# A ring of twenty slots in place of ten for the nodes' own rows in the two source walks

## The reference, cut to what matters

```python
# edge_index = [src, dst]; loops (node, node) are appended to it
h = jax.ops.segment_sum(norm[:, None] * x[col], row, num_segments=num_nodes)
xp = (1.0 - ALPHA) * h + ALPHA * x
```

## Time and profile before

| | |
|---|---|
| median of 3 runs | 5597.37 us (5596.43 to 5601.04) |
| profiled execution, its own time | 5592.3 us |
| its span, from first to last instruction | 5590.6 us |
| e0: first gather to start of the last matmul | 396.0 to 653.1 us |
| e1a: the same | 1015.0 to 1300.5 us |
| e1b: the same | 1302.8 to 1590.6 us |

### The profile page before, as it was taken

One profiled execution on the slowest core, in us unless ns is written; L12 is line 12 of the kernel. 1 busy time (PEld: TensorE's weight loads), 2 busy tenths in 40 slices (PEclk: granted clock), 3 DMA queues, 4 the chain that ended last, 5 costly groups with the idle time before them and its releaser, 6 DMA issues. The chain is left out here.

```text
span 5590.6 us, 101447 instructions
## 1 busy us (share of the span) xinstructions
PE 3616.3 (65%) x21453; PEld 2519.8 (45%) x21454; DVE 3365.2 (60%) x13936; ACT 2238.3 (40%) x6392; POOL 3611.4 (65%) x4923
## 2 busy tenths in 40 slices
PE   4527799777788489968959999930006996200298
PEld 3427688666666244432226666620005775100033
DVE  6434477443468577777758888850806886244288
ACT  0005477666667333323328888700003442000155
POOL 2747566675735377725648888876574555757698
PEclk8659999999999799988979999955558998555699
DMA  1015577687889552200114444352017885411398
GB/s 29 1 33 161 161 240 236 199 244 213 238 241 285 188 196 53 53 18 28 35 59 144 137 144 139 128 153 53 31 41 239 291 290 179 118 34 41 127 342 300
DMA packets 551031, 816.76 MB, mean 146 GB/s; under 512 B 118566, under 2 KB 267629, under 8 KB 550466
## 3 DMA queue, kind: packets, MB, share of 16 engines
q1 hardware_dynamic: 396820, 559.50, 31.8%
q0 software_dynamic: 69184, 122.90, 9.0%
q10 hardware_dynamic: 84816, 132.30, 6.4%
HBM read 493.48 MB, written 329.46 MB: 147 GB/s over the span
## 5 line engine op out<-in xcount | busy, mean ns | idle before, releaser
L620 POOL DMA_INDIRECT agg_dst<-e_rows,e_put_i x392 | 390.3, 996 | 203.8 <-issue 118.8
L1867 POOL DMA_INDIRECT e_rows<-h,e_other_i x392 | 388.6, 991 | 148.5 <-issue 118.8
L1209 POOL TENSOR_TENSOR n_rstd<-n_rstd,minus_half 128x4 f32<-128x4 f32 x294 | 333.5, 1134 | 23.1
L689 POOL DMA_INDIRECT agg<-e_msg,e_put_i x196 | 194.1, 990 | 224.1 <-DVEq L718 172.8
L1222 ACT ACTIVATE n_o<-n_y_ps,n_shift,n_rstd 128x128 f32<-128x128 f32 x784 | 294.5, 463 | 11.6 <-POOL n_shift L1482 11.0
L364 POOL DMA_INDIRECT by_src<-s_pay_s,s_place_i x196 | 188.3, 961 | 112.5 <-issue 58.8
L937 PE MATMUL e1b_bank<-y_rows,e1b_hot 128*128 x1584 | 205.9, 291 | 81.7 <-ACT e1b_bank L1049 58.4
L1683 POOL DMA_INDIRECT lg_rows<-x,e_other_i x196 | 187.5, 956 | 109.7 <-issue 59.4
L895 POOL DMA_INDIRECT x_rows<-x,d_other_i x196 | 185.9, 948 | 112.0 <-issue 59.1
L2366 POOL TENSOR_TENSOR n_u<-n_u 128x512 f32<-128x512 f32 x98 | 124.5, 1270 | 205.2 <-DVE n_u L2313 205.2
L937 PE MATMUL e1a_bank<-y_rows,e1a_hot 128*128 x1584 | 206.4, 291 | 78.3 <-ACT e1a_bank L1035 52.1
(11 more groups left out here) (513 smaller groups left out, 11950.0 us busy)
## 6 DMA issues: line engine op xcount, KB each, us to landing
n_ag<-agg_dst SPq DMA_DIRECT2D x294, 264.0 KB, 3.6
n_xs<-x SPq DMA_DIRECT2D x294, 256.0 KB, 3.4
n_hs<-h SPq DMA_DIRECT2D x196, 264.0 KB, 3.9
agg_dst<-e_ev SPq DMA_DIRECT2D x196, 132.0 KB
y<-n_o ACTq DMA_DIRECT2D x98, 264.0 KB, 3.1
e1a_fed<-y SPq DMA_DIRECT2D x196, 132.0 KB
m<-e1a_ev SPq DMA_DIRECT2D x196, 132.0 KB
e1b_fed<-m SPq DMA_DIRECT2D x196, 132.0 KB
```

The costliest lines, as they stand in the source:

```text
L620: pool.indirect_dma_start(out=agg, out_offset=bass.IndirectOffsetOnAxis(ap=e.put_i[:, c:c + 1], axis=0), in_=rows[:, c, :], in_offset=None ...
L689: pool.indirect_dma_start(out=agg, out_offset=bass.IndirectOffsetOnAxis(ap=e.put_i[:, c:c + 1], axis=0), in_=msg[:, g % SLOTS, k, 0:out_wi ...
L1209: st(pool.tensor_tensor(rstd, rstd, keep.minus_half[:, :], ALU.pow))
L1867: pool.indirect_dma_start(out=rows[:, c, :], out_offset=None, in_=h, in_offset=bass.IndirectOffsetOnAxis(ap=e.other_i[:, c:c + 1], axis=0))\
```

## The change

The ring `fed` gets twenty slots, each with a semaphore of its own, in place of ten. FED stands in the ring's size, in the slot and count of each load and wait, in the number of loads before the loop, and in which tile is asked for after a take.

```diff
-EV, FED = 4, 10
+EV, FED = 4, 20
```

## The result

The changed kernel takes 5535.8 us (median of 4 runs, 5532.5 to 5538.5); the kernel before, run beside it and earlier, 5596.9 (4 runs, 5585.7 to 5601.0). The ratio is 0.9895, interval [0.9879, 0.991]. The two medians are 61.1 us apart; by the ratio the gain is 58.8 us of the 5597, and 48.5 were forecast. The profiled execution takes 5536.55 us after 5592.3, a gain of 55.8.

The account below looks back on a forecast made before the run. The prediction took ACT's waits for tile-row loads, led by only three tiles, to bound e1a and e1b. A ceiling of 59.1 us less 2.6, 6 and 2 gave 48.5, so 5549 us; 8-in-10 range 5537 to 5582.

Parts of the forecast that it names:

- My account of the lateness: Walks e1a and e1b: a load lands in 3.2 us, three tiles of ACT cover 2.5 us, so ACT waits.
- The ceiling of 59.1 us: Most the change could gain: time beyond the gathers, 28.4 us in e1a and 30.7 us in e1b.
- What is lost of it: Parts of the 59.1 us not won in e1a and e1b: 2.6, 6 and 2 us, leaving 48.5.
- the 2.6 us for late landings at the end: Last gathers of e1a and e1b land later beside loads than in e0: 1.3 us lost a walk.
- the 8 us for the middle of the walks: Loss of 6 us from ACT and PE waiting for one another, plus 2 us from e1b's standstills.
- e1b's three stalls: ACT stands still about 4.66 us three times at a turn's end; between nothing and 4.7 us remains, 2 taken.
- What is next behind: After the load waits go, POOL's gathers at 4.99 us a round bound e1a and e1b, ahead of ACT, PE, SP, DMA.
- (a): ACT without load waits: 229 us in e1a, 18 us inside the gathers; 235 us in e1b, 12 inside.
- The forecast of share and rate: DMA engines in the middle of e1a: share 95%, traffic about 267 GB/s, fitting narrowly.
- The rival of full engines: DMA engines already full at a share of 0.86 to 0.88; gain 0 to 10 us, about 5594 us; chance 0.11.
- The eviction ring: Rival: stores landing in 4.07 us make rounds 5.35 us; gain 36 us in all, 5561 us; chance 0.24.
- The burst: Rival: ten more loads at a walk's start delay first gathers, 6.7 us a walk, 5611 us; chance 0.05.

Follow-up runs that it names:

- e1: Changed kernel with twenty slots kept but loads asked for only ten tiles ahead, as before: 6862.7 us against 6864.1, ratio 0.9997 (second kind of chip).
- e3: Ring of 8 slots, so a lead of one tile: 7146.6 us, ratio 1.0411 to the kernel before (second kind).
- e2: Changed kernel with twenty slots but loads asked for twelve tiles ahead, a lead of five: 6846.8 us, ratio 0.9971 to the kernel before (second kind).
- e0: Not a run: the earliest of the kernel's three walks, same sum over as many tiles and chunks as the other two; 260 us in the kernel before.
- e9: Changed kernel, unedited, repeated beside the kernel before on another chip: 5541.0 us against 5595.4, ratio 0.9902 (first kind).
- e4: Changed kernel with ten eviction slots in place of four, in all three walks: 6842.6 us, ratio 0.9968 to the kernel before (second kind).
- e7: Changed kernel with ACT loading the closing values at every second tile in place of every fourth: 6877.9 us, one run (second kind).
- e11: Changed kernel with a lead of five tiles, run once more: 6891.6 us, ratio 0.997 to the kernel before (second kind).
- e12: Changed kernel with ten eviction slots, run once more: 6888.5 us, ratio 0.9968 to the kernel before (second kind).
- e8: Kernel before, with ten eviction slots in place of four: 6899.4 us beside 6896.4, one run (second kind).
- e10: Changed kernel with all 196 gathers of walk e1b left out: 5525.9 us, one run (first kind).
- e5: Changed kernel with half of e1b's gathers left out: 6745.5 us, one run; kernel before 6896.4 (second kind).

## Why the prediction was right, and where not

**What bounded the walks.** Shown. The load of a tile's own rows came late because its lead of three tiles was too short. e1 takes the added lead away and keeps the ring: nothing is won. e3 shortens it: 283 us are lost. e2 stretches it to five: all that a lead can give is there. These three ran only on the second kind, whose walks proper have no gathers beside; on the first kind the cause rests on the traces, in which the load waits and the excess over e0 went together, twice (the result and e9). My account of the lateness left out a part: I set 3.2 us of landing against 2.5 of three tiles. In the earlier trace rows SP issues the load 1.2 us after the start of the take, so it is there after 4.4 us, and ACT is ready for it after 3.1; the 1.3 between them are the wait. e1 shows that the part matters.

**The ceiling of 59.1 us.** It came from the difference of e1a and e1b to e0. The walks now take 258.6 and 260.0 us where e0 took 257.1, so 54.7 were won in the profiled execution and, by the same rows before, 57.1 in e9's.

**What is lost of it.** This is the term that was mis-sized: 10.6 forecast, 4.4 and 2.0 measured. From last gather to the start of the last matmul e1a and e1b now take 13.7 and 15.8 us, where e0 took 12.7; that is 4.1 of the 4.4 us, and 1.6 of e9's 2.0. So the 2.6 us for late landings at the end (3.47 less 2.06 us, twice, is rather 2.8) were about right, and the 8 us for the middle of the walks weren't lost. I gave 3 us a walk to ACT and PE waiting for one another and 2 us to e1b's three stalls. e1b's stalls are still there in the trace after (ACT waits 4.50, 4.66 and 4.78 us, put down to PE, where it waited 4.66, 4.63 and 3.85), and yet e1b gained more than e1a; that the banks in hand and the spare time of a round take them up is my reading, and wasn't tried.

**What is next behind.** Right in kind, wrong in size. I put ACT at 4.5 and PE at 4.53 us a round and called both a tenth below the gathers. Each was the engine by itself, and ACT's from a single round of 4.55. Together, through eight banks and batches of six steps, they make 4.73 in e1a with no gathers (second kind) and 4.86 in e1b (first kind; on the second 4.78 to 4.88 in e2, e4, e7, e11 and e12, which start 477 to 467 ACT instructions from 2100 to 2290 us). The sum in (a) had said so: 229 and 235 us over 49 rounds are 4.67 and 4.80. e7 shows that ACT's own part isn't the limit of that pair; what is, inside it, stays open. e0 is no different: on the second kind its round without gathers is 4.85 to 4.94 us (324 to 330 ACT instructions, two a tile, from 740 to 940 us in e1 to e8). So e0 too, which I called bound by the gathers, is bound by them by only 1 to 3%. A next step that sped up the gathers alone would find 8 us in e1b by e10, and no more.

**DMA.** The forecast of share and rate, 0.95 and 267 GB/s, met 0.93 and 269. The rival of full engines at a share of 0.88 is refuted. The Trainium skill's 358 GB/s (DMA: Bandwidth & Descriptors, Specifications) is 89 above what the walk reached; whether it or the share would have been the wall, no run here shows.

**The eviction ring.** This rival's sign came, with 16.5 and 20.9 us of waits, and its price didn't: the walks end with the gathers. On the second kind ten slots in place of four change nothing (e4 against e2), but there the waits that they remove are 7.0 us, in e1b alone. On the first kind, with 3% of slack, that the waits cost nothing is argued from the walks' lengths and wasn't tried.

**The burst.** Refuted by the trace after: the third batch came 0.6 us earlier.

## What to carry to other kernels

A prefetch must lead by the whole time from the event that frees its issue to its landing, measured against the consumer's fastest burst, not its mean pace: here 1.2 us until SP issues and 3.2 us to land against 0.82 us a tile, where the mean tile took 1.43. Past that, further lead buys nothing: without gathers five tiles did what thirteen did. Beside the gathers five tiles would give 3.1 + 2 x 0.82 = 4.8 us for the 4.4, by my estimate from the earlier trace rows; that wasn't run. So size the lead from the trace and keep the memory. And the pace of two engines that wait for one another isn't that of the slower one alone: take it from a run in which the third is left out, as in e10, before you call a bound clear.

## What the runs showed of the hardware

The same program takes about 5596 us on some chips and 6864 to 6914 on others. In the walks the difference lies in stretches in which POOL issues indirect gathers, and the 35 us behind them: there (e1) PE started 75 matmuls in 200 us where it starts some 1290 without gathers, and ACT and SP fell likewise, while POOL keeps 1.27 us a gather on the mean (1.25 on the first kind); the granted clock of TensorE is 0.50 (its level of 1.2 GHz), with PE busy 27 of the 200 us. Without gathers the pace is that of the first kind (4.78 to 4.88 us a round in e1b, and 4.86 in e10). With half the gathers (e5) the walk was 130 us shorter. By e1's trace the three walks hold 675 of the 1266 us; the rest lies in other phases, which aren't read here. What makes it so stays open; no walk in a trace of the first kind shows any of it. Whoever times a kernel with many gathers should first see which kind of chip it ran on, and then compare two numbers.

A load of 132 KB on SP's queue landed in 3.2 us beside gathers. The Trainium skill's fit for a DMA, 2.0 us plus the bytes over 436 GB/s (DMA: Bandwidth & Descriptors, Anatomy of one DMA), is made for POOL's path and gives 2.3 us for this size, as an estimate; the row is 0.9 us above it at a DMA share of 0.86. Without gathers (e1) the load landed within 2.2 us, at a share of 0.74.
